# One-stage feed-forward units and stored keys and values in a four-batch decoder kernel

## The reference

```
def _mha(x, y, wq, wk, wv, li1_w, ..., causal):
    xn = _ln(x, lnx_g, lnx_b); yn = _ln(y, lny_g, lny_b)
    q, k, v = xn @ wq, yn @ wk, yn @ wv            # 16 heads of 32
    a = softmax(q @ k.T * 32 ** -0.5)              # masked after the softmax if causal
    x_out = x + (a @ v) @ li1_w + li1_b
    h = gelu(_ln(x_out, ln3_g, ln3_b) @ li2_w + li2_b)      # 256 -> 1024
    return x_out + h @ li3_w + li3_b                        # 1024 -> 256

x = _ln(xx, ln1_g, ln1_b)
x = x + _mha(x, x, a1..., causal=True)     # 512 keys
x = _ln(x, ln2_g, ln2_b)
return x + _mha(x, ee, a2..., causal=False)    # ee: the 1024 context rows
```

## Time and profile before

| | us |
|---|---|
| median of 3 runs (lowest, highest) | 4639.05 (4630.34, 4643.46) |
| the profiled execution | 4633.79 |
| its span in the profile | 4632.0 |
| PE busy | 3657.0 (79%) |
| DVE busy | 2278.4 (49%) |
| ACT busy | 1596.6 (34%) |
| POOL busy | 881.5 (19%) |

### The profile page before, as it was taken

How to read it: one execution, slowest core, us unless ns; L and a number is a source line. 1 busy time by engine, 2 the same in 40 slices (tenths; PEclk the granted TensorE clock), 3 DMA queues, 4 the chain that set the end, 5 groups by cost and what they waited for, 6 DMA issues and landing times. The chain is left out here.

```text
span 4632.0 us, 59607 instructions
## 1 busy us (share of the span) xinstructions
PE 3657.0 (79%) x22886; PEld 2035.9 (44%) x22886; DVE 2278.4 (49%) x4385; ACT 1596.6 (34%) x2267; POOL 881.5 (19%) x977
## 2 busy tenths in 40 slices
PE   3887578898887688898886688988886788965995
PEld 2425353435325455245335445244344534244884
DVE  3464755452465754633557663624647664530101
ACT  1342633332342632432344532423435433411221
POOL 0101531101202621011104512011105311012002
PEclk9899689999898789999897799999897799977998
DMA  4110001201200010202100011012100011024444
GB/s 84 35 52 19 1 23 22 59 19 29 76 11 19 1 44 1 59 22 59 48 22 1 1 44 41 18 33 48 52 19 1 1 44 41 18 98 141 172 169 127
DMA packets 240597, 205.30 MB, mean 44 GB/s; under 512 B 111806, under 2 KB 207788, under 8 KB 239916
## 3 DMA queue, kind: packets, MB, share of 16 engines
q1 hardware_dynamic: 232112, 184.36, 14.0%
q0 software_dynamic: 3072, 8.39, 0.6%
q10 hardware_dynamic: 5116, 8.58, 0.6%
HBM read 149.37 MB, written 51.90 MB: 43 GB/s over the span
## 5 line engine op out<-in xcount | busy, mean ns | idle before, releaser
L813 ACT ACTIVATE prob<-psum 128x1024 f32<-128x1024 f32 x384 | 372.2, 1021 | 534.2 <-PE psum L733 534.2
L1143 ACT ACTIVATE prob<-psum 128x1024 f32<-128x1024 f32 (+3 forms) x384 | 331.2, 914 | 443.6 <-PE psum L1063 443.6
L853 DVE TENSOR_REDUCE scr<-psum 128x1 f32<-128x512 f32 x576 | 371.5, 685 | 218.1 <-PE psum L720 213.4
L373 PE MATMUL psum<-ident 128*128 128x128 f32 x3296 | 396.8, 281 | 36.3 <-PEq L69 28.6
L1181 DVE TENSOR_REDUCE stats<-psum 128x1 f32<-128x512 f32 (+3 forms) x576 | 333.7, 619 | 165.0 <-PE psum L1051 160.7
L373 PEld LDWEIGHTS psum<-ident 128*128 128x128 f32 x3296 | 389.5, 197 | 49.2 <-issue 48.1
L1063 PE MATMUL psum<-stack 32*128 32x512 f32 (+3 forms) x1536 | 214.2, 629 | 62.7 <-ACT prob L1143 32.5
L730 PE MATMUL psum<-stack 32*128 32x512 f32 x1536 | 231.6, 673 | 31.2 <-DVE xo L844 24.7
L761 PE MATMUL psum<-prob,ones_f 128*32 128x512 f32 x1536 | 208.1, 609 | 0.0
L1078 PE MATMUL psum<-prob,vbig 128*32 128x512 f32 (+3 forms) x1536 | 194.0, 579 | 4.3 <-ACT prob L1143 4.3
L849 DVE TENSOR_REDUCE scr<-psum 128x4 f32<-128x2048 f32 x48 | 110.0, 2291 | 155.0 <-PE psum L713 155.0
(11 more groups left out here) (417 smaller groups left out, 6739.5 us busy)
## 6 DMA issues: line engine op xcount, KB each, us to landing
ew<-in_L_ffn_W SPq DMA_DIRECT2D x46, 1024.0 KB, 7.6
stack<-q_terms SPq DMA_DIRECT2D x144, 128.0 KB, 2.4
w_mlp<-k_terms SPq DMA_DIRECT2D x72, 256.0 KB, 4.5
w_mlp<-in_L_xattn_a_li_w SPq DMA_DIRECT2D x16, 1024.0 KB, 6.2
q_terms<-parts SPq DMA_DIRECT2D x96, 128.0 KB, 2.1
k_terms<-parts SPq DMA_DIRECT2D x48, 256.0 KB, 3.4
stack<-k_terms SPq DMA_DIRECT2D x72, 128.0 KB, 2.7
k_terms<-parts SPq DMA_DIRECT2D x48, 128.0 KB, 1.9
```

Source lines behind the costliest of these rows:

```text
L373: pe.matmul(psum[:, bank, at:at + P], ident[:, :], ident[:, :], start=True, stop=True, skip_group_check=True)
L813: act.activation(prob[:, i % 4, :, :], psum[:, 2 * p:2 * p + 2, :], ACT.Exp, scale=scale).then_inc(exped, 1)
L853: dve.tensor_reduce(found[:, c:c + 1], ring(i), AX.X, ALU.max).then_inc(freed, 1)
L1143: act.activation(prob[:, i % 4, :, q0:T], psum[:, 2 * p:2 * p + 2, q0:T], ACT.Exp, scale=scale).then_inc(exped, 1)
```

## The change

1. `mlp_unit` is one stage for both units. The 4 row tiles are two halves of 256 rows. The product by li2 for half 0 runs, then the product by li2 for half 1 interleaved with the product by li3 for half 0, then the product by li3 for half 1. Matmuls with li2 are 256 columns wide, where they were 512. For unit 1 the two norms that follow are made per half on DVE, half 0 while half 1 is still being multiplied. There is one `clear` at the end. SP also loads the stored keys and values in unit 1.
2. Keys and values of a2 for all groups are projected in stage "Cq" from the normed context: 16 products on PE, 22 copies on ACT, 6 subtractions on POOL, in the place of the 70 identity matmuls. SP stores terms, keys (2 MB) and values (2 MB) into device memory. POOL waits for all of it at the start of "De", and a barrier is added behind "De". The load of a1's weights moves from stage "Asm" to "De"; "Asm" loads wk and wv of a2.
3. `whole_heads` for a2 projects the queries alone (4 jobs, where there were 20), takes the key terms from device memory, and every second quad from the fourth on uses PSUM banks 0 to 3.

```
-        for w, n in ((w1q, "wq"), (w1k, "wk"), (w1v, "wv")) if i == 1 else ((w2q, "wq"), (w2k, "wk"), (w2v, "wv")):
+        for w, n in ((w1q, "wq"), (w1k, "wk"), (w1v, "wv")) if i == 1 else ((w2q, "wq"),):
...
 whole_heads:
+            jobs = first + of_group(1) + of_group(2) + of_group(3)
...
-                banks_of.append([4, 5, 6, 7])
+                b0 = 0 if terms is not None and u >= HG - 1 and u % 2 else 4
+                banks_of.append(list(range(b0, b0 + 4)))
...
-        in_a_quad, since, asked = 3, 0, 0
+        in_a_quad, since, asked = 3 if terms is None else 2, 0, 0
...
+                if terms is not None:
+                    place_k(1, terms)
+                    place_k(2, terms)
...
-                        pe.wait_ge(taken, 2 + h)
+                        pe.wait_ge(taken, 2 + h if terms is None else 1 if b0 else len(jobs))
...
 mlp_unit, PE:
+            for t in range(QT):
+                join(t)
+            e.keep_running(pe, 8, 5)
+            turn(0, 0, 4)
+            pe.wait_ge(xT_in, KT)
+            pe.wait_ge(e.mlp_loaded, 32)
+            for f in range(FT):
+                rise(0, f)
+                if f == 3:
+                    turn(1, 0, 5)
+            pe.wait_ge(xT_in, 2 * KT)
+            pe.wait_ge(added, QT)
+            for f in range(FT):
+                rise(1, f)
+                for t in HALVES[0]:
+                    fall(t, f)
+            for t in HALVES[1]:
+                for f in range(FT):
+                    fall(t, f)
+            if final is not None:
+                turn(0, 1, 6)
+                e.keep_running(pe, 28, 0)
+                turn(1, 1, 7)
+                e.keep_running(pe, 5, 0)
...
 mlp_unit, DVE, per half behind the product by li3:
+                    ins = dve.tensor_tensor(target[:, t, :], psum[:, FALL[t], 0:C], xo[:, t, :], ALU.add)
+                        last = dve.bn_stats(stats[:, t, :], xa[:, t, :])
+                variance(h)
+                dve.wait_ge(rstd_ready, 3 + 2 * h)
+                    last = dve.scalar_tensor_tensor(xa[:, t, :], xa[:, t, :], mv[:, t, 0:1], gain, ALU.subtract, ALU.mult)
+                    last = dve.scalar_tensor_tensor(xa[:, t, :], xa[:, t, :], rstd[:, t:t + 1], bias_row, ALU.mult, ALU.add)
+                    last = dve.bn_stats(stats[:, t, :], xa[:, t, :])
+                variance(h)
+                normalise(4 + 2 * h, h, xa)
...
 fp6_linear, stage "Cq":
+    jobs = [("k", g, h) for g in (1, 2, 3, 0) for h in range(2)] + [("v", t, 0) for t in range(CT)]
+            for g in range(1, HG):
+                sp.wait_ge(split, 2 * g)
+                sp.dma_start(e.a2_terms[g - 1]...)
+            sp.wait_ge(taken, 2 * HG)
+            sp.dma_start(e.a2_keys, e.work[:, 4096:8192]).then_inc(e.a2_stored, 16)
+            sp.wait_ge(taken, len(jobs))
+            sp.dma_start(e.a2_values, e.work[:, 0:4096]).then_inc(e.a2_stored, 16)
-            e.keep_running(pe, 70, 7)
...
+                pool.tensor_tensor(middle[:, g - 1, half], keys[:, g, half], high[:, g - 1, half],
+                                   ALU.subtract).then_inc(split, 1)
...
 hyperbolic_attention, stage "De":
+            pool.wait_ge(e.a2_stored, 16 * (HG + 1))
             for i in range(2):
                 pool.memset(wide[i][:, :, :, D16:W], 0.0).then_inc(zeros, 1)
...
+    nc.all_engine_barrier(sems_to_clear=range(e.kv_loaded.num, e.a2_stored.num + 1))
```

More of the change, by code:

```diff
@@ L575, in spread_events, with whole_heads @@
         return early, during
-    def whole_heads(tag, q, k, v, V, n_keys, QTg, KTg, MQ, MK, anti=False, wait=None, loading=None):
+    def whole_heads(tag, q, k, v, V, n_keys, QTg, KTg, MQ, MK, anti=False, wait=None, loading=None, terms=None):
         (wq, srcQ), (wk, srcK), wv = q, k, v
@@ L586, in of_group @@
         def of_group(g):
-            return [("q", g, 0)] + [("k", g, h) for h in range(halves)]
+            return [("q", g, 0)] + ([] if terms is not None else [("k", g, h) for h in range(halves)])
         def of_tiles(a, b):
@@ L1332, in load_mlp, with mlp_unit @@
     eng.dma_start(e.w_li3[:, :, :], e.dram[f"L1_xattn_a{i}_li3_w"].rearrange("(k p) n -> p k n", p=P)).then_inc(e.mlp_loaded, 16)
[L1335 to L1337 removed]
+def mlp_unit(e, i, target, storing=None, then_norms=None):
+    nc, psum, ident, R, Ccol = e.nc, e.psum, e.ident, e.R, e.Ccol
     a = f"L1_xattn_a{i}_"
[L1339 to L1361 removed]
@@ L1398, in _ @@
         def _(sp):
[L1399 removed]
+            e.load_kv(sp)
         @block.vector
@@ L1498, in fp6_linear, with _ @@
     sc = [e.vbig[:, i * QT * C:(i + 1) * QT * C].rearrange("p (t n) -> p t n", t=QT) for i in range(3)]
-    with stage(nc, "Cq", "dc", "quant", "turned") as (block, dc, quant, turned):
+    keys = e.work[:, 4096:8192].rearrange("p (g n) -> p g n", g=HG)
+    values = e.work[:, 0:4096].rearrange("p (t n) -> p t n", t=CT)
+    high, middle = (e.parts2[:, :].rearrange("p (g i n) -> p g i n", g=HG - 1, i=2)[:, :, i, :] for i in range(2))
+    jobs = [("k", g, h) for g in (1, 2, 3, 0) for h in range(2)] + [("v", t, 0) for t in range(CT)]
+    with stage(nc, "Cq", "dc", "quant", "turned", "projected", "taken", "split") as (
+            block, dc, quant, turned, projected, taken, split):
+        @block.sync
+        def _(sp):
+            for g in range(1, HG):
+                sp.wait_ge(split, 2 * g)
+                sp.dma_start(e.a2_terms[g - 1].rearrange("i p n -> p i n"),
+                             e.parts2[:, (g - 1) * 2 * TC:g * 2 * TC].rearrange("p (i n) -> p i n", i=2)).then_inc(e.a2_stored, 16)
+            sp.wait_ge(taken, 2 * HG)
+            sp.dma_start(e.a2_keys, e.work[:, 4096:8192]).then_inc(e.a2_stored, 16)
+            sp.wait_ge(taken, len(jobs))
+            sp.dma_start(e.a2_values, e.work[:, 0:4096]).then_inc(e.a2_stored, 16)
         @block.vector
@@ L1507, in _ @@
         def _(pe):
-            e.keep_running(pe, 70, 7)
+            pe.wait_ge(e.kv_loaded, 32)
+            for i, (kind, g, h) in enumerate(jobs):
+                if i >= 4:
+                    pe.wait_ge(taken, i - 3)
+                bank = psum[:, 2 + i % 4, :]
+                if kind == "k":
+                    last = pe.matmul(bank, e.w2k[:, 0, g * P:(g + 1) * P], e.cnT[:, 0, h * BANK:(h + 1) * BANK],
+                                     start=True, stop=True)
+                else:
+                    last = pe.matmul(bank, e.cnT[:, 0, g * P:(g + 1) * P], e.w2v[:, 0, :], start=True, stop=True)
+                last.then_inc(projected, 1)
             pe.wait_ge(quant, 1)
@@ L1516, in _ @@
         def _(act):
+            for i, (kind, g, h) in enumerate(jobs):
+                act.wait_ge(projected, i + 1)
+                bank = psum[:, 2 + i % 4, :]
+                if kind == "v":
+                    act.copy(values[:, g, :], bank).then_inc(taken, 1)
+                    continue
+                half = slice(h * BANK, (h + 1) * BANK)
+                ins = act.copy(keys[:, g, half], bank)
+                if g:
+                    ins = act.copy(high[:, g - 1, half], bank)
+                ins.then_inc(taken, 1)
             act.wait_ge(turned, 1)
             act.copy(e.xT[:, :, :], psum[:, 0:KT, :])
+        @block.gpsimd
+        def _(pool):
+            for i, (kind, g, h) in enumerate(jobs):
+                if kind == "v" or g == 0:
+                    continue
+                half = slice(h * BANK, (h + 1) * BANK)
+                pool.wait_ge(taken, i + 1)
+                pool.tensor_tensor(middle[:, g - 1, half], keys[:, g, half], high[:, g - 1, half],
+                                   ALU.subtract).then_inc(split, 1)
     return e.into_rows(x, x, e.xT, e.wC), e.add_rows(x, e.R["L0_ffn_bias"]), None
```

238 lines of the change are left out of this document (196 added, 42 removed).

## The result

| | before | changed |
|---|---|---|
| median of the runs shown (lowest, highest), us | 4636.8 (4630.3, 4643.5) | 4556.6 (4547.3, 4563.4) |
| the profiled execution's span, us | 4632.0 | 4545.5 |

The ratio is 0.9826, 95% interval 0.9801 to 0.9851: 80 us faster. The forecast was 4597, a gain of 40; the time lies 2 us inside the low end of the range (4555 to 4628), and the gain is twice the one forecast. Windows of the changed kernel, in the order of the earlier trace rows (stretch, length, busy PE, PEld, DVE, ACT, POOL, granted clock, DMA share, GB/s): a batch; the experts; unit 1; the start of attention a2; unit 2 up to the next batch's first work on PE.

The account below looks back on a forecast made before the run. The bound was judged place by place, by whose last work the next stage awaits, in a batch of 1014 us repeated four times. Terms summed to -9.8 us per batch, -39 in all: 4595, stated as 4597, range 4555 to 4628.

Parts of the forecast that it names:

- a Cq without exclusion: Stage Cq: POOL does not delay DVE and PE's clock holds, 9 us less per batch, 4561; within a chance of 0.22.
- Unit 1, -6.3: Unit 1 as one stage: attention a2 starts at 53.7 us where it started at 60.0, -6.3 us per batch.
- Attention a2, -9.4: Start of attention a2: reductions 2.33 us apart from the third on, where they were 3.84; -9.4 us per batch.
- the 0.4 that I gave back for the clock: Start of attention a2: 0.4 us given back for PE's clock, making -9.8 into -9.4 us per batch.
- Unit 2, -3.9: Unit 2: product by li3 ends 4.7 us sooner, the `clear` at the end costs 0.8; -3.9 us per batch.
- Cq, +9.0: Stage Cq and next: POOL's six subtractions delay DVE, +6.5 us, and PE's clock falls, +2.5 us per batch.
- the rival with a cheap Cq: Stage Cq: only DVE's one-input operations wait for POOL, +3.5 us instead of +6.5, 4585; Cq cheaper had chance 0.22.
- The clock's part: Behind PE's pause in Cq, transposes and about half of the next product run at half speed: +2.5 us per batch.
- The barrier behind De: The barrier added behind stage De: +0.8 us per batch.
- the stores that hold POOL: Stores go one at a time and stall DVE in De: +12 us net per batch, 4645 up to 4680; chance 0.07.
- the quads that bring nothing: Start of attention a2: something else holds the overlapping quads, 9.4 us stay, 4635, no change; chance 0.07.
- the clock falls in more places: PE's clock falls at pauses in a2, unit 1 and Cq: +4.5 us per batch, 4615; chance 0.14.

Follow-up runs that it names:

- Run 9: Changed kernel with gain and bias of the norm at the end of unit 1 as operations of their own: 4571.8 us, ratio 0.9864.
- run 8: Changed kernel with unit 1's last two norms made for all four tiles together and 42 identity matmuls ahead of the transposes: 4583.7 us, ratio 0.9879.
- run 4: Changed kernel with all quads of attention a2 in PSUM banks 4 to 7: 4608.3 us, ratio 0.9949.
- run 1: Kernel before with the changed `mlp_unit` alone, without the load of keys and values: 4567.7 us against 4635.1, ratio 0.9856.
- runs 5 and 6: Changed kernel without POOL in Cq: ACT copies the product instead, low-order terms left out, 4529.3 us; or subtraction on PE, same results, 4531.3 us.
- 11: Changed kernel with the subtraction on PE, plus 16 identity matmuls in the stage that loads a batch's rows: 4528.3 us, ratio 0.9762.
- run 3: Changed kernel with 28 identity matmuls behind the 16 products of stage Cq: 4548.5 us, ratio 0.9811.

## Why the prediction came out as it did

The direction held, and with it the reading of which places pay and which one costs. The forecast had half of the gain: several terms of the sum were mis-sized, all to one side, and unit 1 and unit 2 by the most. That the time fell inside the range is luck: its low end was drawn to cover a Cq without exclusion (4561), and the exclusion is real.

- **Unit 1, -6.3, measured -9.5.** The step that failed is "half 0's norms run from 32.2 (its product is done) for about 9 us". That 9 was not worked out operation by operation, though it stood in the sum twice. Counted operation by operation it is two additions and four statistics, two aggregations, two roots, and three passes per tile where before there were four (gain and bias are fused into the scaling): 8.1 us with the waits of 1.13 us for a root, and 7.5 us with the 0.82 measured. Run 9 shows 1.0 us for the fusion, run 8 2.8 us for the halves. I let half 0 end 1.5 us behind the product and half 1 follow with another 9; measured, half 0 ends 0.3 us behind it. The tail behind the last product is 11.3 us where I had 14.0. The remaining 0.9 us is the front: 10.5 instead of 10.9, and products 28.3 instead of 28.8. That makes 3.6 us in the batches whose clock held (60.0 to 50.1); in two others the first product ran at 1.2 GHz, 8.79 us instead of 7.14.
- **Attention a2, -9.4, measured -11.6.** The mechanism was right: run 4 takes the second set of banks away and the gain goes, in part by the clock, which I had not seen in it. Three sizes were off. The period ahead of the third reduction is 3.55 us, not 3.84; the first reduction starts 4.8 us in, not 5.0; a free reduction is 2.22 us, not 2.33. Together that is 1.4 us. And the 0.4 that I gave back for the clock was not due: the first scores ran at 1.2 GHz before as well. The last 0.4 lies behind the first scores, in code that didn't change.
- **Unit 2, -3.9, measured -6.9.** Three sizes of 1 us each. By unit 1's working the last product by li3 was to end 4.7 us sooner; at the same clock it ends 5.6 sooner (38.8 us behind the stage's start, before 44.4). I carried the product by li1 over at 8.83 us, from the one batch of the earlier trace rows. Before the change it took that in three of the four batches, and in the second

```profile
2039.29 7.14 PE L445 MATMUL psum<-w_li,yT 128*128 128x256 f32 x32 [1.93 <-PEq L1326]
```

behind the same pause of 1.93 us. In the changed kernel it takes 7.1 in all four, in run 1 8.8 in all four, which is most of the 2.2 us between those two. So the reading that a pause of 1.9 us put the clock down doesn't hold in every batch, and why it held here isn't shown. And the 0.8 for the `clear` doesn't appear: from the last product by li3 to the next batch it is 12.1 us, before 12.3.

- **Cq, +9.0, measured +6.7.** The exclusion is real: runs 5 and 6 take POOL away and DVE is back at 17.4 us. Its price was 5.15 us, not 6.5. One subtraction delays DVE by 0.86 us and not by nearly its 1.15. The row that I read said so already: 0.65 us of POOL's time were left and 0.96 of DVE's own would have made 1.61, and the operation took 1.46. It strikes one-input operations (0.69 to 1.53) as much as two-input ones (1.23 to 2.06), so the rival with a cheap Cq by the Trainium skill's "Advanced Engine Details and Errata" (VectorE Performance Modes) failed. DVE's two-input operations were held too, as the Trainium skill's "GPSIMD Engine Reference" (Key points) has it. The clock's part was as forecast in the first batch: PE's work is 3.2 us longer (0.9 and 2.3), the path 2.5 (0.9 in the transposes, 1.6 in the stage behind, 11.1 to 12.7 us). But in the other three the kernel before had already lost 0.9 us in the stage behind Cq, its product at 5.38 us. I had read one batch only.
- **De and the stores.** The stores cost nothing, as forecast; I had compared with 77 GB/s for one and 116 over a window, and together they went at up to 437. The barrier behind De is 0.4 us or less, not 0.8.
- **The rest, 0, measured -1.1**, with self attention -2.7, a1 -1.9, hyperbolic attention +1.0 and the batch's first stages +2.5. All go with microseconds at 1.2 GHz, in code that the change doesn't touch; that the one is the cause of the other wasn't tested.
- **The last sum.** 4595 and the 5 us of the median make 4600, not 4597; that took 3 us off the miss.

Of the rivals, the stores that hold POOL and the quads that bring nothing are refuted by the trace. That the clock falls in more places is half right: it falls at the start of unit 1 in two batches and for longer in Cq, but for less time in a2 and unit 2, and in the sum of the table there are 223 us at 1.2 GHz per batch where there were 219.

What stays open is what makes the clock of one stage depend on how the stages ahead of it lie. Runs 8, 9 and 11 show that 1 to 3 us of work moved in one stage change others by as much; no run here tells the rule.

## What to carry to other kernels

A chain that stands on the path more than once deserves a sum operation by operation, from the operations of the changed code; a round number there costs more than all the fine terms around it. Where PE works in another engine's shadow, that work may be what holds its clock: taking it out pays only if the pauses go too, as the second set of banks shows. And a subtraction of two SBUF operands on POOL is not free beside DVE; if PE has room, a matmul by minus the identity into the bank that already holds the product does it without POOL, 21 to 25 us here. Last, read every batch and not the first alone: a product that took 8.83 us in one took 7.14 in the next.

## What the runs showed of the hardware that was not expected

- One POOL operation of 1.15 us beside DVE costs DVE 0.83 to 0.97 us and itself takes 11.01 / 6 = 1.83 us; the two took turns, one operation each.
- With quads of 1.14 us and pauses of 2.4 us PE's granted clock went to 0.50 and stayed there for 37 us, so that the quads took 2.09 us and one set of banks cost 13.7 us per batch where 6.7 were expected at full clock.
- Identity matmuls behind a pause cost more than they hold: 34 of them 10.5 us instead of 7.7. Where they filled a pause from its beginning (run 3) the clock held in that stage.
- The same pause of 1.93 us ahead of the same product was followed by 1.2 GHz in three batches and by 2.4 GHz in the fourth.
